# A transformer decoder layer on one core: a rebuilt order of its steps, normalisations on GpSimd, and the mask added by VectorE under the row maxima

## What is computed

```python
x = x + self_attention(layernorm(x))            # softmax(q k^T / sqrt(8) + bias of i - j) v
x = x + cross_attention(layernorm(x), ctx, mask)  # where mask == 0 a score is -1e9
x = x + ffn(layernorm(x))                       # silu(gate) * up, 512 wide
# each product of the ffn has ternary weights and rows rounded to 8-bit steps of their maximum
```

## Time and profile before

| | us |
|---|---|
| median of 3 runs | 514.28 |
| the runs | 513.12, 514.28, 520.25 |
| span of the profiled execution | 513.4 |

### The profile page before, as it was taken

One profiled execution on the slowest core, in us unless ns is written; L12 is line 12 of the kernel. 1 busy time (PEld: TensorE's weight loads), 2 busy tenths in 40 slices (PEclk: granted clock), 3 DMA queues, 4 the chain that ended last, 5 costly groups with the idle time before them and its releaser, 6 DMA issues.

```text
span 513.4 us, 18365 instructions
## 1 busy us (share of the span) xinstructions
PE 454.1 (88%) x5596; PEld 328.0 (64%) x5596; DVE 398.0 (78%) x1154; ACT 372.9 (73%) x993; POOL 254.6 (50%) x691
## 2 busy tenths in 40 slices
PE   2246889999999999999999999999999999997762
PEld 1224556777777777777777777777777777764440
DVE  5722446799888889888888988889888888877553
ACT  0222556788888888888888888888888887775451
POOL 4221445655565555555566655555556654434110
PEclk9999789999999999999999999999999999999785
DMA  6264255555455545454445555544454555223000
GB/s 186 77 192 107 72 143 142 140 142 141 134 134 144 141 122 145 139 135 131 122 138 135 135 128 135 137 135 122 133 137 137 137 137 136 79 86 92 23 7 10
DMA packets 82191, 62.48 MB, mean 122 GB/s; under 512 B 57634, under 2 KB 71714, under 8 KB 82146
## 3 DMA queue, kind: packets, MB, share of 16 engines
q1 hardware_dynamic: 82146, 61.92, 44.4%
HBM read 46.47 MB, written 14.88 MB: 119 GB/s over the span
## 4 chain that ended last, share of the span: by engine, by line
PE 78%; DVE 5%; DMA 4%; issue 4%; SPq 3%; ACT 3%; POOL 1%; DVEq 0%; POOLq 0%; ACTq 0%
PE bank L1117 14%; PE bank L1092 12%; PE bank L1059 11%; PE bank L1088 6%; PE bank L1055 6%; PE bank L1264 4%; PE bank L1210 3%; PE bank L1138 2%; PE bank L1237 2%; PE bank L1175 2%; PE bank L1154 2%; PE bank L1295 2%; PE bank L1303 2%; PE bank L1224 2%; PE bank L1196 2%
## 5 line engine op out<-in xcount | busy, mean ns | idle before, releaser
L533 ACT ACTIVATE probs<-bank 128x512 f32<-128x512 f32 x256 | 145.5, 597 | 32.0 <-PE bank L1092 31.7
L826 DVE TENSOR_REDUCE neg_max_S<-bank 128x4 f32<-128x512 f32 x128 | 87.1, 685 | 34.3 <-PE bank L1059 34.2
L826 DVE TENSOR_REDUCE neg_max_X<-bank 128x4 f32<-128x512 f32 x128 | 84.2, 676 | 8.9 <-PE bank L1059 5.7
L1059 PE MATMUL bank<-stack_k_S,stack_q_S 120*128 120x128 bf16 x512 | 46.9, 227 | 12.9 <-DMA stack_k_S<-scratch_S 12.4
L432 POOL TENSOR_TENSOR qk_rest_X<-qk_X,qk_parts_X 128x256 f32<-128x256 f32 x32 | 21.4, 670 | 70.8 <-ACT qk_parts_X L536 70.8
L1092 PE MATMUL bank<-stack_q_S,stack_k_S 122*128 122x128 bf16 x512 | 52.5, 229 | 4.5 <-DMA stack_q_S<-neg_maxT_S 4.5
L1117 PE MATMUL bank<-probs,v_aug_S 128*32 128x128 f32 x1024 | 55.5, 291 | 0.0
L1055 PE MATMUL bank<-mask_bias,ident_bf 128*128 128x512 bf16 x128 | 49.4, 386 | 3.6 <-issue 2.3
L1092 PEld LDWEIGHTS bank<-stack_q_X,stack_k_X 74*128 74x128 bf16 x512 | 40.6, 99 | 16.4 <-issue 1.6
L1092 PE MATMUL bank<-stack_q_X,stack_k_X 74*128 74x128 bf16 x512 | 50.8, 222 | 0.0
L1088 PE MATMUL bank<-ident_bf,mask_bias 128*128 128x512 bf16 x128 | 50.3, 393 | 0.0
(11 more groups left out here) (159 smaller groups left out, 1159.1 us busy)
## 6 DMA issues: line engine op xcount, KB each, us to landing
stack_q_S<-scratch_S SPq DMA_DIRECT2D x32, 288.0 KB
stack_k_S<-scratch_S SPq DMA_DIRECT2D x96, 96.0 KB
stack_q_X<-scratch_X SPq DMA_DIRECT2D x32, 288.0 KB
stack_k_X<-scratch_X SPq DMA_DIRECT2D x96, 96.0 KB
scratch_S<-qk_parts_S SPq DMA_DIRECT2D x32, 192.0 KB, 2.3
scratch_X<-qk_parts_X SPq DMA_DIRECT2D x32, 192.0 KB, 2.3
ctx_in<-ctx SPq DMA_DIRECT2D x32, 64.0 KB, 2.7
mask_in<-mask SPq DMA_DIRECT2D x32, 64.0 KB, 1.8
```

Source lines behind the costliest of these rows:

```text
L533: act.activation(probs[:, c, :], bank_b[c % 2][:, :], ACT.Exp).then_inc(sems["exp_" + a], 1)
L826: dve.tensor_reduce(neg_max[a][:, first_head(c):first_head(c) + 2 * HC - 1:2], bank_a[c % 2][:, :].rearrange("i (h j) -> i h j", h=HC), AX ...
L1059: last = pe.matmul(bank[:, part_of_bank(hh)], stack_q[a][rows, p, head(c, hh)], stack_k[a][rows, p, head(c, hh)], start=not masked, stop=n ...
```

## The change

The loop is gone: all 47 steps (t from -1 to 45) are written out, with constant counts. Each engine's order in a step and its lags are new, and the lags are now counted per engine (SyncE's by five steps later than TensorE's, ScalarE's and VectorE's partly by one earlier). TensorE's lags among themselves are those of before plus one, but for the front of X, which comes one step later, and V, which is projected together with queries and keys. What else changes:

- `scores_a` of X has no masking matmul (BIASED names all four banks). Instead VectorE's `row_max` of X issues 16 `tensor_tensor_reduce` a batch, one for each head: it reads the head's 128 scores in PSUM and the 128 bf16 values of the mask's bias, writes minus their sum to `biased` (bf16, read by nobody), and the minimum of it to one column of `neg_max`. `scores_b` keeps its masking matmul.
- `normalise` of S, X and F and `quantise_y` are GpSimd's. GpSimd also makes the negated mean (`negate_mean`, one column).
- The context comes transposed from the host and is loaded straight into `ctxT`; the transpose, its copy and `ctx_in` are gone.
- probs and o_raw are separate for S and X; V has four copies instead of two; `xnT_ps_X` goes to bank_o.
- The four `attend` of S follow each other. `max_transposed` transposes 128 columns, of which 96 are zero.

The core of the diff; helpers otherwise keep their work, and `users` lists who last used a bank:

```diff
-FRONT_S, A_S, B_S, FRONT_X, A_X, B_X, POST_X, FFN2 = 0, 2, 3, 4, 5, 6, 7, 8
-CTX_T = 3
-V_S = 1
-LN_S = -1
-DEPTH = 8
-UNROLL = 4
-LOOP_FROM, LOOP_TO = 10, 30
+STEPS = [(t, t) for t in range(-1, B + 14)]
...
+V_COPIES = 4
+BIASED = (0, 1, 2, 3)
...
-        ctx_in = sb("ctx_in", [S, 2, D])
-        probs = sb("probs", [S, CH, HC * S])
-        o_raw = sb("o_raw", [128, 2, S])
+        probs = {a: sb(f"probs_{a}", [S, CH, HC * S]) for a in "SX"}
+        o_raw = {a: sb(f"o_raw_{a}", [128, 2, S]) for a in "SX"}
+        neg_mean = {k: sb(f"neg_mean_{k}", [S, 1]) for k in "SXF"}
+        biased = sb("biased", [S, CH, HC, S], BF16)
+        XNT_BANK = {"S": bank_s, "X": bank_o}
...
-        def value(eng, count):
-    return count if isinstance(count, int) else eng.to_reg(count)
-        def run(eng, step):
-    for t in range(LOOP_FROM):
-        step(Step(0, t))
-    with eng.Fori(0, (LOOP_TO - LOOP_FROM) // UNROLL) as turn:
-        for t in range(UNROLL):
-            step(Step(turn, LOOP_FROM + t))
-    for t in range(LOOP_TO, B + DEPTH):
-        step(Step(0, t))
+        def done(b, per=1, upto=None):
+    return b * per + (per if upto is None else upto)
+        def loaded(b, per):
+    return (b // 2 + 1) * per
+        def after(eng, st, *users):
+    for name, lag, *signal in users:
+        stage = name[-1] if name[-2:] in ("_S", "_X") else "F"
+        b = st.of(stage, lag)
+        if b is not None:
+            eng.wait_ge(sems[name], done(b, CH, signal[0]) if signal else done(b))
+            return
+        def run(step):
+    for s, x in STEPS:
+        step(Step(s, x))
...
+        sp.dma_start(ctxT[:, b % 2, :], ctx[b]).then_inc(sems[f"ctx_loaded{b % 2}"], 16)
...
+    def negate_mean(k, st, lag):
+        b = st.of(k, lag)
+        if b is None or (k == "S" and b == 0 and st is not START):
+            return
+        pool.wait_ge(sems["mv_" + k], done(b))
+        if b:
+            pool.wait_ge(sems["xn_" + k], done(b - 1))
+        pool.tensor_scalar(neg_mean[k][:], mv[k][:, 0:1], -1.0, None, ALU.mult)\
+            .then_inc(sems["neg_mean_" + k], 1)
...
+    def normalise(k, st, lag):
+        b = st.of(k, lag)
+        if b is None or (k == "S" and b == 0 and st is not START):
+            return
+        pool.wait_ge(sems["neg_mean_" + k], done(b))
+        pool.wait_ge(sems["rstd_" + k], done(b))
+        if k != "F" and b:
+            pool.wait_ge(sems["xnT_ps_" + k], done(b - 1))
+        if k == "F" and b:
+            pool.wait_ge(sems["amax_y"], done(b - 1))
+        pool.tensor_scalar(xn[k][:], x_all[:, b, :], neg_mean[k][:, 0:1], rstd[k][:, 0:1],
+                           ALU.add, ALU.mult).then_inc(sems["xn_" + k], 1)
+    def quantise_y(st, lag):
+        b = st.of("F", lag)
+        if b is None:
+            return
+        pool.wait_ge(sems["y_inv"], done(b))
+        if b:
+            pool.wait_ge(sems["yT_ps"], done(b - 1))
+        pool.tensor_scalar(y_q[:], xn["F"][:], y_inv[:, 0:1], ROUND16, ALU.mult, ALU.add)\
+            .then_inc(sems["y_q"], 1)
...
+        if a == "X" and c in BIASED:
+            if c == BIASED[0]:
+                dve.wait_ge(sems["mask_bias"], done(b))
+                if b:
+                    dve.wait_ge(sems["max_X"], done(b - 1, CH))
+            for hh in range(HC):
+                head = first_head(c) + 2 * hh
+                last = dve.tensor_tensor_reduce(biased[:, c, hh, :], quarter(bank_a[c % 2], hh), mask_bias[:, b % 2, :],
+                                                -1.0, -2.0 * BIG, ALU.add, ALU.min,
+                                                neg_max[a][:, head:head + 1])
+            last.then_inc(sems["max_" + a], 1)
+            return
...
+        masked = a == "X" and c not in BIASED
+        if masked:
+            pe.wait_ge(sems["mask_bias"], done(b))
+            pe.matmul(bank[:, :], ident_bf[:], mask_bias[:, b % 2, :].unsqueeze(1).to_broadcast([S, HC, S]),
+                      start=True, stop=False)
+        for hh in range(HC):
+            last = pe.matmul(bank[:, part_of_bank(hh)], stack_q[a][rows, b % 2, head(c, hh)],
+                             stack_k[a][rows, b % 2, head(c, hh)], start=not masked,
+                             stop=not masked or hh == HC - 1)
+        last.then_inc(sems["score_a_" + a], 1)
...
+    def project_qkv(a, st, lag, *users):
+        b = st.of(a, lag)
+        if b is None:
+            return
+        pe.wait_ge(sems["xnT_" + a], done(b))
+        if a == "X":
+            pe.wait_ge(sems[f"ctx_loaded{b % 2}"], loaded(b, 16))
+        after(pe, st, *users)
+        queries = xnT[a][:, b % 2, :]
+        keys = queries if a == "S" else ctxT[:, b % 2, :]
+        pe.matmul(quarter(bank_p, 0), w_qkv[a][:, 0, :], queries, start=True, stop=True)
+        pe.matmul(quarter(bank_p, 1), w_qkv[a][:, 1, :], keys, start=True, stop=True)
+        pe.matmul(quarter(bank_p, 2), keys, w_qkv[a][:, 2, :], start=True, stop=True)\
+            .then_inc(sems["qkv_ps_" + a], 1)
```

More of the change, by code:

```diff
@@ L54, with __init__, of @@
 X_CUTS = (0, 2, 8, B)
-WARM = 4
+WARM, WARM_BATCHES = 4, 4
+BIASED = (0, 1, 2, 3)
 STACK_LOADS = 3 * len(REL_PAIRS) + 2
[L59 to L80, removed]
-class Step:
[L86 to L91, removed]
+class Step:
+    def __init__(self, s, x):
+        self.first = {"S": s, "X": x, "F": x}
+    def of(self, stage, lag):
+        first = self.first[stage]
+        return first - lag if first is not None and 0 <= first - lag < B else None
+START = Step(0, None)
 def layer(nc, x, ctx, mask, w_self, w_cross, w_ffn, w_down, cols, w_out_s, w_out_x, bo_rows,
@@ L373, in _ @@
+                store(st, 14)
+                mask_load(st, 10)
+                stack_in("X", st, 10)
+            run(step)
             sp.wait_ge(sems["out_stored"], 16 * B)
@@ L554, in xnT_out @@
[L554 to L566 removed]
+                act.wait_ge(sems["av_" + a], done(b, CH))
@@ L567, in xnT_out, with qk_out @@
                     .then_inc(sems["xnT_" + a], 1)
-            def ctxT_out(st, b):
-                if not b:
+            def qk_out(a, m, st, lag):
+                b = st.of(a, lag)
+                if b is None:
                     return
-                act.wait_ge(sems["ctxT_ps"], b.count())
-                if b.before(2):
-                    act.wait_ge(sems["v_ps_X"], b.before(2).count())
-                copy(ctxT[:, b.parity, :], quarter(bank_s, 1)).then_inc(sems["ctxT_ready"], 1)
@@ L703, in _ @@
+                exp("S", st, 3, 0)
+                exp("S", st, 3, 1)
+                maxT_out("X", st, 6)
+                xnT_out("X", st, 4)
+                exp("S", st, 3, 2)
+                oT_out("X", st, 7)
+                exp("S", st, 3, 3)
+                qk_out("X", 0, st, 4)
+                qk_out("X", 1, st, 4)
+                quantise_h(st, 8)
+            run(step)
         @block.vector
@@ L995, in _ @@
+                row_max("X", st, 6, 2)
+                row_max("X", st, 6, 3)
+            run(step)
         @block.tensor
@@ new lines, in scores_a, with scores_b @@
+                last.then_inc(sems["score_a_" + a], 1)
+            def scores_b(a, st, lag, c, *users):
+                b = st.of(a, lag)
+                if b is None:
+                    return
+                bank, rows = bank_b[c % 2], slice(0, A_ROWS[a] + M_ROWS)
+                after(pe, st, *users)
+                if c == 0 and a == "S" and b < WARM_BATCHES:
+                    keep_warm(bank)
+                if c == 0:
+                    pe.wait_ge(sems[f"max_in_{a}{b % 2}"], loaded(b, 16))
@@ L1053, in scores_a @@
                 masked = a == "X"
                 if masked:
[L1055 removed]
+                    pe.matmul(bank[:, :], mask_bias[:, b % 2, :], ident_bf[:].unsqueeze(1).to_broadcast([S, HC, S]),
                               start=True, stop=False)
[L1057 removed]
                 for hh in range(HC):
[L1059 to L1061 removed]
@@ L1094, in scores_b, with attend @@
+                    last = pe.matmul(bank[:, part_of_bank(hh)], stack_k[a][rows, b % 2, head(c, hh)],
+                                     stack_q[a][rows, b % 2, head(c, hh)], start=not masked,
                                      stop=not masked or hh == HC - 1)
                 last.then_inc(sems["score_b_" + a], 1)
-            def attend(a, st, b, c):
-                if not b:
+            def attend(a, st, lag, c, *users):
+                b = st.of(a, lag)
+                if b is None:
```

1171 lines of the change are left out of this document (512 added, 659 removed).

## The result

| | before | after |
|---|---|---|
| median of four runs each, us | 515.43 | 541.73 |
| lowest and highest | 513.12, 520.25 | 540.8, 546.81 |
| span of the profiled execution | 513.4 | 539.0 |

The prediction said 496 (480 to 528) and faster; the kernel became slower, and the time lies outside the range.

What follows compares the result with a forecast made beforehand. TensorE bounds the kernel before, VectorE the new one. Full steps gain 15.4 us and the loop 2.8, together 18.2 off the 513.4 span: 495.2, plus 0.9 for the median gives 496, range 480 to 528.

Steps and rivals of the forecast that it cites:

- What bounds the kernel before: Full steps: TensorE is busy throughout the 13.24 us step, with VectorE 1.4 us behind it and ScalarE 1.7.
- Loop, 2.8: Loop turns: five steps of 13.80 us become 13.24 when written out, a gain of 2.8 us.
- TensorE, 11.85 a step: TensorE's step: masking matmuls, context transpose and attend spacing take 1.39 off 13.24, leaving 11.85 us; clock near 1.00.
- VectorE, 0.27 a combined instruction: VectorE's row maxima of X: sixteen at 0.27 us add 4.32, making its step 11.96 us and VectorE fullest.
- rival C: VectorE's combined instruction: readout stands alone, 0.32 us each, step stays 13.2, only the loop gains; 511 us, chance 0.13.
- 7.64: VectorE's step of 11.82 us less 4.18 for the removed row maxima, normalisations and y's quantising.
- Rival E: VectorE's sixteen combined instructions run serially at 0.41 us each, step 14.6; slower, 544 us, chance 0.17.
- GpSimd, 10.2 to 11.0 a step and 0 in cost: GpSimd's added instructions: 2.4 to 3.2 us more a step, still under the other engines, costing nothing in full steps.
- the self-attention's parts go out two places later: SyncE's queue: the later store, with ctx loaded straight to ctxT and no added DMA, costs 0.
- Waits, 0: Full steps: scores_a's longer wait is covered by other TensorE work, and separate buffers remove no visible wait; 0.
- Entry and drain, 0 (−6 to +5): Start and end of the run: chain savings and added hand-overs about cancel, drain has room; 0, bounds −6 and +5.
- Full step 12.6: Full steps: VectorE's 11.96 us with 0.6 left idle gives 12.6 against 13.24 before; chance 0.42.

Runs made afterwards that it cites:

- kernel 9: kernel 5 with X's stack load split: the queries' load before the self-attention's store, the three key loads after it; 490.09 us, ratio 0.9482.
- kernels 5: The changed kernel with one SyncE line moved, so the self-attention's parts go out ahead of the X stacks again; 503.26 us, ratio 0.9812.
- experiment 8: kernel 3 with only the three normalisations and y's quantising moved from VectorE to GpSimd, all queue orders as before; 542.08 us, ratio 1.0561.
- Experiments 4: The kernel before with two SyncE lines exchanged, so the self-attention's parts go out after the X stacks; 535.7 us, ratio 1.0415.
- kernel 3: The kernel before with its hardware loop written out and nothing else changed; 508.02 us, ratio 0.9832.

## Why the prediction was wrong, step by step

*What bounds the kernel before:* right. Written out, TensorE is busy 99.5 of 100 us in it.

*Loop, 2.8:* right in sign, too small; 7.1. I compared only the step at a turn with its neighbours, so what the loop cost every step could not show; and only four full steps, not five, have the 13.8.

*TensorE, 11.85 a step:* right or a little high. In kernel 9 it is busy 91.93 of 100 us, and at 12.35 a step that is 11.35. Its clock didn't stay at 1.00 in the changed kernel, since it idles there; in kernels 5 and 9 it did, in 200 to 400 us.

*VectorE, 0.27 a combined instruction:* mis-sized, 0.21. The readout costs nothing in the stream. The rule of rival C, that such an operation is two instructions ("VectorE: DVE Perf Modes" of the Trainium skill, section on two Vector instructions with no wait between them), is in the trace; its estimated price of 0.32 isn't, nor is C's 0.32. The sum with 0.21 is 7.64 + 3.36 = 11.00; kernel 9 shows 92.85 of 100, 11.47 at its step, below the 11.96 forecast. Where the 0.47 above the sum lie was not traced.

*Rival E's serial instruction, 0.41:* fell, though its 544 lies 2 us from the result. A time that agrees says nothing of the mechanism.

*GpSimd, 10.2 to 11.0 a step and 0 in cost:* the load is right (81.93 of 100, 10.1), the prices too (0.45, 0.37 and 0.24 against 0.46 to 0.66 and 0.19). The cost of 0 is wrong in the old order: 34 us in experiment 8, with no engine full. In the rebuilt order this part was not taken out alone, so what it costs or gives there is open.

*SyncE, "the self-attention's parts go out two places later. No DMA is added. 0.":* this is the step that failed. I counted DMAs and bytes and didn't lay the queue out in time. What the store was moved behind is X's stack, one place in the order but four DMAs and 2.9 us of issue, which lay between the store and its reload and hid the landing. Behind them the landing is open, for S by 2.1 us and for X by 2.2, and SyncE's round of 9.7 becomes 13.95, longer than TensorE's 11.4. Experiments 4 and 5 show it from both sides: the swap costs the kernel before 20 us, and undoing it gives the changed one 38. All that was needed stood in the trace of before: the queue's times, and the 2.3 us that a store takes to land.

*Waits, 0:* wrong with SyncE's; the four separate buffers weren't tried alone.

*Entry and drain, 0 (−6 to +5):* +1.9 and +6.7 in the changed kernel, −3.7 and +1.9 in kernel 5, within the bounds once the queue is repaired.

*Full step 12.6:* what the arithmetic gives without SyncE's hole. Kernel 5 has 12.61, with a span of 494.5 against my 495.2. Part of that agreement is luck: the loop was worth 4 us more, and TensorE's 22.4 us of waiting for maximum rows took up what the cheaper combined instruction may have given. And the profiled run is the fastest of five: the median, 503.26, lies further above its span than the 0.9 I had added. Beside kernel 3, which has only the loop written out and takes 508.02, kernel 5 is not clearly faster: the intervals of the two ratios overlap.

## What to carry to other kernels

Lay the queue that issues the DMAs out in time as you would an engine: when a store and its reload share it, what stands between them is the cover of the landing, and moving a line without adding a byte can become the bound. When no engine is full after a change, look for the round that only waits for itself; steps of equal length in kernels of different arithmetic give it away. A move of work between engines is to be judged with the order it comes with: here both moves lose alone in the old order (10 and 34 us), while in the new one, with the store in its place, the mask's gains 12. Measure against the right neighbour, too: beside the kernel that only has its loop written out, the whole change is level even with the store in its place, and is ahead, by 18 us, only with the stack split around it.

## What was not expected of the hardware

- The readout of the accumulator (0.08 us) runs beside the next combined instruction; independent ones behind each other start 0.21 apart though each lasts 0.28 to 0.29.
- After an idle of 3.1 us TensorE was granted 0.91 for the first 1.4 us, 0.51 for the next 3.2, then 1.00; seven idles of 1.7 to 3.1 us in 200 to 400 us went so. For TensorE an idle costs more than its length, and the price comes after work has begun again.
- A store of 192 KB lands in 2.3 us before the loads of a stack are queued and in 4.0 behind them.
- A hardware loop of four steps costs 0.2 to 0.3 us in each step of a full TensorE, besides 0.56 at four of its five turns; where in the step the 0.2 lies was not looked for.
- The same normalisation, 128 by 128 in f32, takes VectorE 0.35 us for X and F and 0.70 for S in kernel 3; why is open.
